# Sums of weight blocks by accumulating transfers, and token columns stored by pair

## What is computed

```python
x = x + tanh(g_xattn) * xattn(layernorm(x), ctx, mask, wq, wk, wv, wo, q_norm_w, k_norm_w)
#   32 query heads, 8 key/value heads of 128; q and k are RMS-normalised; softmax in fp32
x = x + tanh(g_ffn) * ffn(layernorm(x), A, B, Wr)
#   scores = x @ Wr.T; softmax over the top 16 of 64 experts; sum over experts of gate * B(A x), rank 16
```

## Time and profile before

| | us |
|---|---|
| median of 3 runs (2540.65 to 2543.59) | 2540.8 |
| the profiled execution's own time | 2547.66 |
| its span | 2545.8 |
| TensorE busy in the span | 2323.6 (91%) |
| VectorE, ScalarE, GpSimd busy | 1680.2, 1178.5, 1511.4 |

### The profile page before, as it was taken

How to read it: one execution, slowest core, us unless ns; L and a number is a source line. 1 busy time by engine, 2 the same in 40 slices (tenths; PEclk the granted TensorE clock), 3 DMA queues, 4 the chain that set the end, 5 groups by cost and what they waited for, 6 DMA issues and landing times.

```text
span 2545.8 us, 35745 instructions
## 1 busy us (share of the span) xinstructions
PE 2323.6 (91%) x11384; PEld 1929.5 (76%) x11384; DVE 1680.2 (66%) x2631; ACT 1178.5 (46%) x3731; POOL 1511.4 (59%) x2134
## 2 busy tenths in 40 slices
PE   5998996999999989999999799999998998878899
PEld 4886884888777778887888688788787876666687
DVE  6656556777677787766777835755757877454755
ACT  4545554556565676655666722322324234232321
POOL 6877557777677767766765344644655665334431
PEclk8999998999999999999999799999999998989899
DMA  4767565444444464444432544546455578564753
GB/s 175 252 200 256 157 219 170 121 133 132 130 133 129 120 224 133 133 133 133 133 104 86 182 160 152 198 156 211 162 166 199 182 215 273 148 227 128 242 174 140
DMA packets 329770, 427.69 MB, mean 168 GB/s; under 512 B 16240, under 2 KB 238704, under 8 KB 317552
## 3 DMA queue, kind: packets, MB, share of 16 engines
q1 hardware_dynamic: 329584, 425.39, 52.3%
HBM read 275.91 MB, written 149.42 MB: 167 GB/s over the span
## 4 chain that ended last, share of the span: by engine, by line
PE 41%; POOL 24%; DMA 20%; issue 7%; DVE 5%; SPq 2%; ACT 1%; POOLq 0%; ACTq 0%; DVEq 0%
PE bank L773 13%; PE bank L775 13%; PE bank L774 13%; DMA mini_combo<-in_sets 9%; DMA combos<-mini_combo 4%; POOL s_hi L1730 4%; POOL staged L1720 2%; POOL staged L1724 2%; POOL staged L1718 2%; DVE s_lo L1276 2%; POOL mini_combo L1808 2%; DMA gates_of_ranks<-gates_t 2%; POOL mini_combo L1805 1%; POOL mini_combo L1810 1%; POOL mini_combo L1806 1%
## 5 line engine op out<-in xcount | busy, mean ns | idle before, releaser
L773 PE MATMUL bank<-t_hi,s_hi 128*128 128x512 f32 x2720 | 1116.4, 410 | 120.6 <-DVE s_lo L1276 50.1
L775 PE MATMUL bank<-t_hi,s_lo 128*128 128x512 f32 x2720 | 1081.4, 398 | 0.0
L774 PE MATMUL bank<-t_lo,s_hi 128*128 128x512 f32 x2720 | 1080.0, 397 | 0.0
L1276 DVE TENSOR_TENSOR s_lo<-staged,s_hi 128x512 fp32r<-128x512 f32 x676 | 571.1, 888 | 211.8 <-ACT s_hi L1007 148.6
L773 PEld LDWEIGHTS bank<-t_hi,s_hi 128*128 128x128 f32 x2720 | 523.5, 192 | 236.8 <-issue 85.7
L775 PEld LDWEIGHTS bank<-t_hi,s_lo 128*128 128x128 f32 x2720 | 522.0, 192 | 116.2
L774 PEld LDWEIGHTS bank<-t_lo,s_hi 128*128 128x128 f32 x2720 | 524.7, 193 | 94.8
L1007 ACT CAST s_hi<-staged 128x512 fp32r<-128x512 f32 x452 | 260.5, 622 | 428.8 <-DMA staged<-heads 194.8
L1718 POOL TENSOR_TENSOR staged<-staged 128x512 f32<-128x512 f32 x96 | 136.4, 1421 | 305.7 <-DMA staged<-gated 104.3
L1386 DVE SCALAR_TENSOR_TENSOR probs<-bank,small,mask 128x128 f32<-128x128 f32 x512 | 144.0, 343 | 163.3 <-POOL small L1710 109.1
L1101 ACT ACTIVATE probs<-probs,small 128x128 f32<-128x128 f32 x512 | 198.0, 387 | 53.5 <-DVE small L1390 52.5
(11 more groups left out here) (124 smaller groups left out, 3225.8 us busy)
## 6 DMA issues: line engine op xcount, KB each, us to landing
heads<-heads SPq DMA_DIRECT2D x128, 256.0 KB, 3.7
t_raw<-combos SPq DMA_DIRECT2D x24, 1024.0 KB, 9.0
staged<-in_w_q SPq DMA_DIRECT2D x32, 768.0 KB, 5.7
staged<-heads SPq DMA_DIRECT2D x32, 768.0 KB, 5.9
t_raw<-in_sets SPq DMA_DIRECT2D x22, 1024.0 KB, 8.8
mini_combo<-in_sets SPq DMA_DIRECT2D x80, 256.0 KB, 3.4
combos<-mini_combo SPq DMA_DIRECT2D x80, 256.0 KB, 2.3
sums<-sums SPq DMA_DIRECT2D x18, 1024.0 KB, 7.9
```

Of the source, the lines that this page charges most:

```text
L773: nc.tensor.matmul(out[:, :], s_hi[w][:, cols], t_hi[k][:, at, :], start=start, stop=False, skip_group_check=True)
L774: nc.tensor.matmul(out[:, :], s_hi[w][:, cols], t_lo[k][:, at, :], start=False, stop=False, skip_group_check=True)
L775: done = nc.tensor.matmul(out[:, :], s_lo[w][:, cols], t_hi[k][:, at, :], start=False, stop=at == 3, skip_group_check=True)
L1276: return nc.vector.tensor_tensor(out, whole, hi.bitcast(FP32), ALU.subtract)
```

## The change

1. The sums of weight blocks no longer pass through SBUF or GpSimd's arithmetic. Per set, SP copies blocks inside HBM (two transfers of 2 MB), then GpSimd issues three transfers that add to HBM in place: one of 2 MB, two of 1 MB, each after the one before has landed. The four steps of set 1 are in entries 1 to 4, those of sets 2 to 6 in query entries 18 to 39 but 31 and 32, one step per entry. The copies are issued in slot 3, the adding transfers in slot 2 behind `sums`. All of `mini`, `mini_in`, `mini_out`, `combo_in`, `combo_out` goes.
2. The sums are now only additions; signs move to the stationary sums and the results (`minus`, `from_bank`), with the same number of operations of the same shapes.
3. `xt` and `x2t` are laid out by pair, in runs of 2 KB. SP stores `xo` with one transfer of 1.75 MB. The store of `xo2` is one such transfer too, issued by GpSimd right behind line 1784, one beat earlier than SP did.
4. TensorE reads the moving operand of the token sets in four runs of 128 columns, 512 apart.

```diff
-        self.xt = scratch("xt", 2, 7, P, 4, 4, S)
+        self.xt = scratch("xt", 2, 7, 4, P, HALF)
...
+    def combo_steps(e):
+        if 1 <= e <= 4:
+            return [(1, e - 1)]
+        return [(2 + u // 4, u % 4) for u, n in enumerate(n for n in range(2, 24) if n not in (15, 16)) if e == QA0 + n]
...
-                    sp.wait_ge(xt_out, 448 * (tau - 1))
-                src = d.xt[tau - 2, k].rearrange("p k a c -> p k (a c)")
+                    sp.wait_ge(xt_out, 64 * (tau - 1))
+                src = d.xt[tau - 2, k].rearrange("a p c -> p a c")
...
+                if k == 0:
+                    sp.wait_ge(combo_added, 48 * which)
...
+        def combo_copies(e):
+            for which, step in combo_steps(e):
+                if step == 0:
+                    if which > 1:
+                        sp.wait_ge(combo_added, 48 * (which - 1))
+                    sums, raw = d.combos[which].rearrange("b p c -> p b c"), d.sets[which].rearrange("b p c -> p b c")
+                    sp.dma_start(sums[:, 0:2, :], raw[:, 0:2, :]).then_inc(combo_copied, 16)
+                    sp.dma_start(sums[:, 2:4, :], raw[:, 0:4:2, :]).then_inc(combo_copied, 16)
...
-            for k in SEVEN:
-                sp.dma_start(d.xt[u // 4, k, :, :, u % 4, :], xo[:, k, :, :]).then_inc(xt_out, 16)
+            sp.dma_start(d.xt[u // 4, :, u % 4].rearrange("k p c -> p k c"), xo[:, :, :, :].rearrange("p k b q -> p k (b q)")).then_inc(xt_out, 16)
...
-                if at == 11:
-                    sp.wait_ge(fo_pool, 2 * f + 2)
-                    for k in SEVEN:
-                        sp.dma_start(d.x2t[p // 4, k, :, :, p % 4, :], xo2[:, k, :, :]).then_inc(ft_out, 16)
...
-                if u is not None:
-                    mini_in(u)
-                if (n, r) == (30, 0):
-                    mini_out(79)
+                if r == 3:
+                    combo_copies(e)
...
+            if entry.tau in TOKEN_SETS:
+                out = out.rearrange("p (a c) -> p a c", a=4)
+                high = t_hi[k][:, :, at * P:at * P + P]
+                low = t_lo[k][:, :, at * P:at * P + P]
...
-            plus(ev[:, :], usum[:, :], 2)
+            from_bank(ev[:, :], 2, usum[:, :])
...
+        def combos(e):
+            for which, step in combo_steps(e):
+                sums, raw = d.combos[which], d.sets[which]
+                if step == 0:
+                    continue
+                if step == 1:
+                    pool.wait_ge(combo_copied, 32 * which)
+                    to, part = sums[2:4].rearrange("b p c -> p b c"), raw[2:4].rearrange("b p c -> p b c")
+                if step == 2:
+                    pool.wait_ge(combo_added, 48 * which - 32)
+                    to, part = sums[0], sums[3]
+                if step == 3:
+                    pool.wait_ge(combo_added, 48 * which - 16)
+                    to, part = sums[1], sums[0]
+                nc.gpsimd.dma_start(to, part, accum_op=ALU.add, max_dma_last_dim=8192).then_inc(combo_added, 16)
...
+                    pool.wait_ge(fo_pool, 2 * i + 2)
+                    p = 7 - i
+                    nc.gpsimd.dma_start(d.x2t[p // 4, :, p % 4].rearrange("k p c -> p k c"),
+                                        xo2[:, :, :, :].rearrange("p k b q -> p k (b q)")).then_inc(ft_out, 16)
```

More of the change, by code:

```diff
@@ L58 @@
 TAUS = 11
+TOKEN_SETS = (2, 3, 8, 9)
 FILL_POSITIONS = (4, 5, 6, 7, 9, 10, 11)
@@ L671, in _ @@
                     values_out(e, 0)
-                    if combo_unit(e + 1) is not None and e < 15:
-                        combo_in(combo_unit(e + 1), pc)
+                    combo_copies(e)
                 if j == 6 and e and e % 2 == 0:
@@ L772, in part @@
             start = k < 4 and at == 0
-            nc.tensor.matmul(out[:, :], s_hi[w][:, cols], t_hi[k][:, at, :], start=start, stop=False, skip_group_check=True)
-            nc.tensor.matmul(out[:, :], s_hi[w][:, cols], t_lo[k][:, at, :], start=False, stop=False, skip_group_check=True)
-            done = nc.tensor.matmul(out[:, :], s_lo[w][:, cols], t_hi[k][:, at, :], start=False, stop=at == 3, skip_group_check=True)
+            out, high, low = out[:, :], t_hi[k][:, at, :], t_lo[k][:, at, :]
+            if entry.tau in TOKEN_SETS:
+                out = out.rearrange("p (a c) -> p a c", a=4)
+                high = t_hi[k][:, :, at * P:at * P + P]
+                low = t_lo[k][:, :, at * P:at * P + P]
+            nc.tensor.matmul(out, s_hi[w][:, cols], high, start=start, stop=False, skip_group_check=True)
+            nc.tensor.matmul(out, s_hi[w][:, cols], low, start=False, stop=False, skip_group_check=True)
+            done = nc.tensor.matmul(out, s_lo[w][:, cols], high, start=False, stop=at == 3, skip_group_check=True)
             if at == 3:
@@ L1290, in plus, with minus, from_bank @@
             return nc.vector.tensor_tensor(out, a, bank[BANK_OF[k]][:, :], ALU.add).then_inc(taken[BANK_OF[k]], 1)
+        def minus(out, a, k):
+            return nc.vector.tensor_tensor(out, a, bank[BANK_OF[k]][:, :], ALU.subtract).then_inc(taken[BANK_OF[k]], 1)
+        def from_bank(out, k, a):
+            return nc.vector.tensor_tensor(out, bank[BANK_OF[k]][:, :], a, ALU.subtract).then_inc(taken[BANK_OF[k]], 1)
         def second_product(e):
@@ L1309, in result22 @@
             dve.wait_ge(taken[2], plan.after[e, 2])
-            plus(out, ev[:, :], 3)
+            minus(out, ev[:, :], 3)
         def result12(e, out):
             dve.wait_ge(prod, plan.prod[e, 5])
-            plus(out, usum[:, :], 5)
+            from_bank(out, 5, usum[:, :])
         def result21(e, out):
@@ L1717, in sums @@
             pool.wait_ge(st_in, 16 * (plan.order[e] + 1))
-            nc.gpsimd.tensor_tensor(staged[:, 2, :], staged[:, 3, :], staged[:, 6, :], ALU.add).then_inc(s_sum, 1)
+            nc.gpsimd.tensor_tensor(staged[:, 2, :], staged[:, 3, :], staged[:, 6, :], ALU.subtract).then_inc(s_sum, 1)
             pool.wait_ge(s_sum, at + 1)
@@ L1723, in sums @@
             pool.wait_ge(s_sum, at + 2)
-            nc.gpsimd.tensor_tensor(staged[:, 5, :], staged[:, 4, :], staged[:, 1, :], ALU.subtract).then_inc(s_sum, 1)
+            nc.gpsimd.tensor_tensor(staged[:, 5, :], staged[:, 4, :], staged[:, 1, :], ALU.add).then_inc(s_sum, 1)
         def fill_s(e, ks):
@@ L1795, in add_sums @@
                 pool.wait_ge(taken[1], plan.after[e, 1])
[L1796 to L1797 removed]
+                for at, sign in ((1, ALU.subtract), (2, ALU.add)):
+                    nc.gpsimd.tensor_tensor(acc[b][:, at, :], acc[b][:, at, :], usum[:, :], sign).then_inc(o_sum, 1)
             if j == 3:
@@ L1826, in _ @@
         pool.wait_ge(t0_combo_pool, 1)
-        nc.gpsimd.tensor_tensor(t_raw[6][:, :, :], b21_again[:, :, :], t_raw[1][:, :, :], ALU.subtract).then_inc(t0_combo_pool, 1)
+        nc.gpsimd.tensor_tensor(t_raw[6][:, :, :], b21_again[:, :, :], t_raw[1][:, :, :], ALU.add).then_inc(t0_combo_pool, 1)
         for e in range(KV0, QA0):
             for j in SEVEN:
-                if j == 1 and combo_unit(e) is not None:
-                    combos(combo_unit(e), pc)
+                if j == 4:
+                    combos(e)
                 if j == 2 and e:
```

105 lines of the change are left out of this document (23 added, 82 removed).

## The result

The changed kernel takes 2461.4 us (median of 4 runs, 2459.7 to 2462.2) against 2540.8: ratio 0.968, 95% interval 0.967 to 0.970. It is 3.1% faster, where I forecast 2.1%. The time is inside the range, but it is that of the rival "all is hidden" (2459), not that of the case I held likeliest. Its profiled execution took 2460.9 us with a span of 2459.1, so it stands at its own median; that of before stood 6.9 us above. The spans are 86.7 us apart.

A forecast was written before the change was run, and what follows sets the result against it. Entries 18 to 44 were taken as bound by the pieces' order on GpSimd. 2547.7 - 56 - 13 + 12 + 0 + 1 + 7 - 4 = 2494.7, less 6.9 for the profiled execution: 2488 us, range 2445 to 2540.

The forecast's parts named there:

- all is hidden, D: Whole kernel: copies under 18 us, entries at 29.4, entry 17 at floor; 2459 us, or 2450; chance 0.16.
- What bounds the kernel: Entries 18 to 44: bound by the pieces' order, VectorE waiting for GpSimd and GpSimd for loads, not by arithmetic or bandwidth.
- Pieces out of entries 18 to 44, -56: 25 entries, without 31 and 32, fall from 801.1 us to 745, 29.8 each; ends -26 and -66.
- Entries 16 and 17, -13: Entry 17 falls from 41.8 to about 31 us, entry 16 keeps nearly all; ends -5 and -20.
- The copies, +12: SP's queue: 22 us of copies per set make heads' store and staged tile late, 2.4 us five times; 0 to +150.
- The adding transfers, 0: Query entries: GpSimd's issues and landings of the fifteen transfers are hidden; up to +75.
- KV, +1: KV entries: earlier refills -2, copies in entry 1 ahead of the next staged tile +3; -2 to +20.
- The store in the last slice, +7 and -4: Entries 76 to 81: GpSimd's 3.0 us issue exceeds 1.9 slack, +7; SP's queue freed in entry 81, -4.
- A: SP's queue: copies of 49 us per set delay heads' store and staged tile; 2645 us; chance 0.11.
- B: Query entries stay at 31.0 us, TensorE's waits being VectorE's own order; 2518 us; chance 0.14.
- C: Last slice: GpSimd's store issue costs 5.7 us, 2504 in all, or 9 us, 2524; chance 0.11.

The follow-up runs named there:

- experiments 3 and 4: Kernel before, sums of sets 2 to 6 not formed: pieces' arithmetic only 2462.3 us, loads and stores only 2464.3; then arithmetic twice without those transfers, 2503.2.
- no_sums_2_to_6: Changed kernel without any copy or adding transfer for sets 2 to 6, so their sums are not formed: 2456.4 us.
- transfers_old_columns: Changed kernel with the old layout of the token columns, seven SP transfers per pair, for x and the second layernorm: 2465.3 us.
- best_one: Changed kernel with SP storing the last slice's columns, set 1's copies behind entry 1's staged loads, its adding transfers in entries 3, 4, 5: 2444.5 us.

## Why the prediction was right and wrong

- **What bounds the kernel.** Right that the 27 query entries were long because VectorE waits for GpSimd and GpSimd for its pieces, and that the floor was entry 45's. Wrong in the cause in full: I read the 178 us of load waits as the cost. They and the 142 us of arithmetic fell on one budget of 270 us, and either alone costs nothing in these entries (experiments 3 and 4). The forecast did not suffer, since the change removes both.
- **Pieces out of entries 18 to 44, -56.** -66.1 in the 25 entries, 29.4 each against the 29.8 that I took, and so the low end that I gave. The half microsecond that I kept for entry 44's 30.6 was not there: that entry was only catching up. Entries 31 and 32, which I had kept, gave 2.3 more. The sign that I gave for the stretch, 812 us, is not my own sum, which makes 816, and 828 with the term for the copies.
- **Entries 16 and 17, -13.** -21.6. Entry 16 lost 5.3 and entry 17 16.4, to 25.5 us, below the 29.3 of its successors; I had taken 31 from those, though entry 17 has less of the attention woven in (142 matmuls in the changed kernel, against 176 in entry 19). In entry 17 the clock came back too, from 0.80 to 1.00, with the stall gone.
- **The copies, +12: the mis-sized term.** At most 2 us. Threshold about right (18.3 worked out for the heads, 19 to 20 measured by doubling; the staged tile's 20 was not tested by itself), duration wrong: 16 to 18.4 us, not 22. My nearest row counted the latency of four transfers in sequence; I said so and took off only 2 of its 24 us. The estimate from the Trainium skill, "DMA: Bandwidth & Descriptors", section "Latency and other measured facts" (207 to 214 GB/s in each direction for copies between HBM tensors, of another layout than here; hence 20 us), was too long as well; the rows decide.
- **The adding transfers, 0.** Right: `no_sums_2_to_6` shows at most 2 us in the stretch, and GpSimd never waits for their landing. The 19.4 us that it waits for values beside them I had not foreseen; they fall within its spare time.
- **KV, +1.** +5.2. I priced the copies in front of the staged tile at 3 us, by time on the queue; the landing 10.4 us after its issue made GpSimd stand 8.3, and the next staged load met the adding transfer, which I had looked at only for the query entries. That is the step in which I failed to apply my own reason where it did bite. Of the -2 for an earlier refill, entry 8 did give 2.1 us, but it gives 3.2 with seven stores per pair too (`transfers_old_columns`, 28.7 against 31.9), so not for my reason.
- **The store in the last slice, +7 and -4.** -0.9. Right that the issue stands on GpSimd's path: given back to SP it saves 7.1 us in six entries. The size was off (1.05 us, with its wait 1.34, against 3.0) and so was the slack: GpSimd had none. Wrong that the path through the landing keeps its length: it fell by 1.7 us per entry and paid for the issue. Of the -4 for SP's queue, entries 82 and 83 gave 1.6 us, no more than they differ between other kernels here.
- **The rest, 0.** Right: the other entries lost 1.0 us together. The floor of a query entry is 29.31 us with the moving operand read in four runs of 128 columns and without (`transfers_old_columns`).
- **Rivals.** A's mechanism is real, but needs copies longer than some 19 us: at 29 it took 46 us of the gain of 79, with the keys' load in it beside the heads' store. B fell: the entries reached 29.3. C fell: 1.05 us. D is what happened, but that its 2459 lies 2 us from the time is in part luck: KV cost 4.2 us more than its sum has, the last slice 3.9 less.

Summed, the spans' difference is 33.7 us larger than the 53 forecast: 24.4 in entries 18 to 44, 8.6 in 16 and 17, 3.9 in the last slice, 1.0 elsewhere, less 4.2 in KV. By the medians the gain is 79.4 us, 26.4 more than forecast. The other 7.3 are no part of the change: the profiled execution of before stood 6.9 us above its median, that of the kernel after 0.4 below, so the differences by entry are some 7 us too large in all, and where those lie no run shows.

## What to carry to other kernels

An engine in program order has a budget per iteration: add its operations and its waits for round trips, and hold the sum against what it would otherwise spend waiting for slower engines. In entries 18 to 44 here the operations alone and the waits alone were free, both together lengthened the entries by about what they stood above the budget, and taking away either half brought the whole gain. Look at the entries at the stretch's edge by themselves: in 16 and 17 each half cost something alone. Work moved to the queues costs little until it stands ahead of a load that is due: put a long transfer behind the next due load, not in front, and check this in every stretch where it is issued. If a loop's period doesn't move, look whether two paths of equal length have changed places: here undoing one half of an edit gave what the other half had gained.

## What was unexpected of the hardware

- Copies inside HBM run as fast as loads into SBUF do: the doubled copies land 6.4 us apart for 2.10 MB each, some 330 GB/s read and as much written, while the refill of entry 31 moved 345 GB/s.
- GpSimd's issue of a transfer costs 0.87 us for 128 rows of 8 KB, 1.2 us for 256 such rows and 1.05 us for 896 runs of 2 KB. So over these three it does not follow the number of runs. SP's issue of the same columns in seven transfers took 5.66 us.
- Transfers that add in place take 8.5 us for 1 MB from issue to landing and 13.9 for 2 MB, 16.0 at the longest; SP's first copy of 2 MB takes 10.8.
- The clock fell with the stalls: over entry 3 it is 0.88 with the stall and 1.00 without (`best_one`), over entry 19 0.87 with doubled copies and 1.00 without, over entry 17 0.80 before and 1.00 after. The 28 or 29 matmuls of line 745 in entry 3 took 12.3 us of busy time in place of 11.1, so part of what such a stall costs is the slower clock.
